# Grouping the products that prepare keys, queries and values in a decoder kernel on one core

## The reference, cut to what matters

```python
# self-attention, 16 heads of 8 features, causal band of 64, relative bias
attn = softmax(where(mask, q @ k.T * scale, -1e30) + bias); y = (attn @ v) @ w_proj.T + b_proj
x = layernorm(x + y)
# cross-attention, 16 heads of 64 features, keys rotated by cos and sin
q = LN(x) @ Wq; k, v = split(LN(ctx) @ Wkv); k = rope(k, cos, sin)
x = layernorm(x + softmax(clip(q @ k.T * scale, -11, 11)) @ v @ Wo + bo)
```

## Time and profile before

| | us |
|---|---|
| median of 3 runs | 1079.42 |
| lowest and highest | 1076.92 and 1081.24 |
| the profiled execution, its own time | 1080.22 |
| its span in the trace | 1078.5 |
| busy: TensorE, VectorE, ScalarE, GpSimd | 932.1, 686.1, 513.8, 503.9 |
| main phase, first `unit(0)` to the start of the last `unit(1)` | 88.7 to 831.4 |
| mean granted clock over the span | 0.938 |

### The profile page before, as it was taken

One profiled execution on the slowest core, in us unless ns is written; L12 is line 12 of the kernel. 1 busy time (PEld: TensorE's weight loads), 2 busy tenths in 40 slices (PEclk: granted clock), 3 DMA queues, 4 the chain that ended last, 5 costly groups with the idle time before them and its releaser, 6 DMA issues.

```text
span 1078.5 us, 22081 instructions
## 1 busy us (share of the span) xinstructions
PE 932.1 (86%) x8504; PEld 660.6 (61%) x8504; DVE 686.1 (64%) x1905; ACT 513.8 (48%) x1446; POOL 503.9 (47%) x637
## 2 busy tenths in 40 slices
PE   3658998999899899989999998999989589999932
PEld 2436665666666666666656665666656379888721
DVE  3355657767776765777577658757689634444467
ACT  3645563565466456536645663564334023333324
POOL 1034356536644653565465456446567211333354
PEclk9989899999999999999999999999999669999955
DMA  7100000000000000000000000000000001222211
GB/s 180 28 1 6 11 1 2 5 12 1 6 11 1 2 6 11 1 7 11 2 1 6 11 2 1 1 2 1 21 1 1 1 7 25 32 33 32 32 12 40
DMA packets 60422, 15.09 MB, mean 14 GB/s; under 512 B 41230, under 2 KB 59678, under 8 KB 60190
## 3 DMA queue, kind: packets, MB, share of 16 engines
q1 hardware_dynamic: 60318, 13.69, 6.0%
HBM read 10.51 MB, written 3.17 MB: 13 GB/s over the span
## 4 chain that ended last, share of the span: by engine, by line
PE 63%; DVE 18%; ACT 7%; POOL 5%; issue 3%; DMA 2%; SPq 2%; POOLq 0%; DVEq 0%
PE score_banks L1906 9%; PE out_bank L1830 8%; PE score_banks L1637 5%; PE bank_a L1618 5%; DVE o_rec L1238 4%; PE score_banks L1844 4%; PE score_banks L1662 3%; DVE prob L1336 3%; PE bank_d L1713 3%; PE score_banks L1639 3%; PE score_banks L1638 3%; PE score_banks L2034 3%; PE out_bank L1813 2%; PE out_bank L1838 2%; PE bank_d L2047 2%
## 5 line engine op out<-in xcount | busy, mean ns | idle before, releaser
L914 ACT ACTIVATE prob<-score_banks 128x1024 f32<-128x1024 f32 x128 | 131.2, 1025 | 165.1 <-PE score_banks L1906 164.8
L694 POOL TENSOR_TENSOR psum<-psum,prob 128x512 f32<-128x512 f32 x64 | 81.7, 1276 | 155.0 <-DVE prob L1336 154.9
L1906 PE MATMUL score_banks<-qh,kr 64*128 64x256 f32 x1024 | 150.1, 413 | 1.7 <-ACT qh L873 1.3
L1238 DVE RECIPROCAL o_rec<-out_bank 128x256 f32<-128x256 f32 x64 | 111.9, 1748 | 26.2 <-PE out_bank L1838 26.2
L692 POOL TENSOR_TENSOR psum<-prob 128x512 f32<-128x512 f32 x64 | 82.9, 1295 | 95.2 <-DVE prob L1336 95.0
L1830 PE MATMUL out_bank<-prob,v 128*64 128x256 f32 x1024 | 124.6, 385 | 1.4 <-DVE on L1239 1.4
L1906 PEld LDWEIGHTS score_banks<-qh,kr 64*128 64x128 f32 x1024 | 91.2, 191 | 40.5 <-issue 30.9
L845 ACT ACTIVATE prob<-prob,neg_max 128x128 f32<-128x128 f32 (+1 forms) x256 | 107.0, 426 | 12.9 <-DVE neg_max L1138 12.9
L1336 DVE TENSOR_SCALAR prob<-prob 128x1024 f32<-128x1024 f32 x128 | 100.5, 785 | 12.9 <-ACT prob L914 12.9
L1830 PEld LDWEIGHTS out_bank<-prob,v 128*64 128x64 f32 x1024 | 67.8, 136 | 46.6 <-issue 17.2
L963 ACT ACTIVATE prob<-score_banks 128x8 f32<-128x8 f32 x255 | 45.3, 178 | 97.5 <-PE score_banks L2034 97.5
(11 more groups left out here) (384 smaller groups left out, 2115.4 us busy)
## 6 DMA issues: line engine op xcount, KB each, us to landing
cb<-in_ctx_dram SPq DMA_DIRECT2D x8, 256.0 KB, 2.9
bias_mask<-bias_scratch SPq DMA_DIRECT2D x1, 1536.0 KB, 7.3
xb<-in_x_dram SPq DMA_DIRECT2D x8, 128.0 KB, 2.1
prob<-in_L_xattn_Wkv_dram SPq DMA_DIRECT2D x1, 1024.0 KB, 7.2
x_scratch<-v SPq DMA_DIRECT2D x16, 64.0 KB, 1.5
bias_mask<-x_scratch SPq DMA_DIRECT2D x16, 64.0 KB
att_scratch<-on SPq DMA_DIRECT2D x16, 64.0 KB, 1.5
prob<-att_scratch SPq DMA_DIRECT2D x16, 64.0 KB, 3.0
```

The costliest lines, as they stand in the source:

```text
L914: s.activation(prob[:, p % 2, 2 * u:2 * u + 2, :].rearrange("p k (h q) -> p h k q", h=2), sc[:, 0:2, :].rearrange("p h (k q) -> p h k q", ...
L1238: link(w.reciprocal(o_rec[:, :], bank[:, T:2 * T]))
L1906: last = mm(sc[:, h, k * T:(k + 1) * T], kr[rows_of, p % 2, kb * P:(kb + 1) * P], qh[rows_of, p % 2, :], start=True, stop=True, skip_group ...
```

## The change

`GROUPED` names the pairs 0, 1, 2, 4, 5 and 6. In these, TensorE issues `keys b` directly behind `keys a` in the first half, and in the second half `queries`, `values 0` and `values 1` directly behind one another, with the slots 2 to 5 after them. VectorE does the sine product of `keys b` ahead of `attended`. ScalarE copies both values behind the queries and ahead of the slots 2 to 5. `prep_targets` numbers the jobs in the new order, which deals the banks anew. Pairs 3 and 7 stay. No instruction is added or removed.

```diff
--- before.py
+++ after.py
@@ -84,6 +84,9 @@
     return job
 
 
+GROUPED = (0, 1, 2, 4, 5, 6)
+
+
 def prep_targets(p, last):
 
     target = {}
@@ -91,9 +94,12 @@
         return {} if last else {"keys a": 1, "values 0": 0, "values 1": 0, "queries": 0, "keys b": 1}
     if p + 2 < PAIRS or not last:
         target["keys a"] = (p + 2) % PAIRS
-    target["queries"] = p + 1
+    if p not in GROUPED:
+        target["queries"] = p + 1
     if p + 2 < PAIRS or not last:
         target["keys b"] = (p + 2) % PAIRS
+    if p in GROUPED:
+        target["queries"] = p + 1
     if p % 2 == 1:
         target["values 0"] = target["values 1"] = (p + 1) // 2
     return target
@@ -934,7 +940,11 @@
                         slots(4, 6)
                     if (b, p, "queries") in JOB:
                         queries(JOB[b, p, "queries"])
-                    if p < PAIRS - 1:
+                    if p in GROUPED:
+                        values_job(0)
+                        values_job(1)
+                        slots(2, 6)
+                    elif p < PAIRS - 1:
                         slots(2, 4)
                         values_job(0)
                         slots(4, 5)
@@ -1348,11 +1358,14 @@
                     clamp(0)
                     slots(0, 1)
                     slots(1, 2)
+                    if p in GROUPED:
+                        keys_job("b")
                     if pair >= 1:
                         attended(pair - 1)
                     clamp(1)
                     slots(2, 3)
-                    keys_job("b")
+                    if p not in GROUPED:
+                        keys_job("b")
                     slots(3, 4)
                     slots(4, 5)
                     if p == 0 and b >= 1:
@@ -1929,13 +1942,20 @@
 
                     unit(0)
                     prep("keys a", prep_keys, "a")
+                    if p in GROUPED:
+                        prep("keys b", prep_keys, "b")
                     slots(0, 1)
                     if pair >= 1:
                         values_of(pair - 1)
                         sum_of(pair - 1)
                     slots(1, 2)
                     unit(1)
-                    if p < PAIRS - 1:
+                    if p in GROUPED:
+                        prep("queries", prep_queries)
+                        prep("values 0", prep_values, 0)
+                        prep("values 1", prep_values, 1)
+                        slots(2, 6)
+                    elif p < PAIRS - 1:
                         prep("queries", prep_queries)
                         slots(2, 3)
                         prep("keys b", prep_keys, "b")
```

## The result

The changed kernel takes **1094.87 us** (median of 4 runs, 1094.31 to 1095.27), the kernel before beside it 1079.44 (1076.92 to 1081.24): a ratio of 1.0152 with an interval of 1.013 to 1.0175. It is 15.4 us slower, as forecast (1096.5 within 1085 to 1106). The profiled execution took 1095.27 us, with a span of 1093.6 us against 1078.5.

A forecast was written before the change was run, and what follows sets the result against it. TensorE was taken to bound the kernel, busy 932.1 of 1078.5 us. Pairs sum to 3.0 us a batch, +21 for seven; 1080.2 + 21 − 2 − 2 = 1097.2, median 1096.5 us, range 1085 to 1106.

The forecast's parts named there:

- First halves +0.70: Every grouped pair before unit(1): the three products of keys b moved there add 0.70 us.
- Pair 1: VectorE sets the pace; subtraction and sine product delay slot 10, its wait splits: net +0.2 us, bounds −0.4 to +0.5.
- Pair 2: Slot 16's turn waits for ScalarE's copy, so only 0.1 us comes back in the second half: net +0.6 us.
- Pair 4: Keys b were hidden in slot 27's wait for ScalarE's copy, so nothing comes back: net +0.7 us, bounds +0.5 to +0.7.
- Pair 5: ScalarE's copies of values delay the chain through slot 32 and the division to slot 35: net +1.5 us, bounds +0.7 to +1.9.
- First and last batch −2: Last batch: moved keys b end a 0.89 us wait; first batch: longer pair 1 waits absorb some; −2 us for both.
- Clock −2: Shorter or split waits in pairs 7 and 1 win back a third of 6.0 us lost at half clock: −2 us.
- The rival "faster": Grouping removes ten border penalties of 0.1 us, 1.0 us a batch, all gained: 1072.5 us, chance 0.05.
- The clock recovers: Rival: all half-clock stretches vanish since no wait lasts 2 us: 1090 us, chance 0.15.
- The clock falls: Rival: pair 1 idles 3.0 us instead of 2.1, some 4 more batches lose 1.5 us each: 1103 us, chance 0.13.
- No difference: Rival: the added 0.7 us is absorbed in the other pairs as in pair 6: about 1081 us, chance 0.07.
- GpSimd's sum is later: Rival: pair 7's second addition waits for pair 6's clamp, behind the sine product: +0.65 us a batch, 1101 us, chance 0.10.

The follow-up runs named there:

- experiment 5: The changed kernel with fewer pairs grouped: 0, 1 and 6 (1068.65 us), 1 alone, 1 and 6, or 0, 1, 4 and 6 (8.8 us above the first).
- experiment 4: The changed kernel with ScalarE copying pair 5's values behind slot 33, TensorE's order untouched: 1094.45 us, ratio 1.0132 to the kernel before.
- experiment 2: The changed kernel with keys b still early, but slots back between queries and values, differing in pairs 1 and 5: 1115.77 us, ratio 1.0319 to the kernel before.
- experiment 3: The kernel before with keys b of pairs 0, 2 and 4 directly behind the queries in the second half: 1091.35 us, ratio 1.0102.

## Why the prediction was right

**Sign, size and mechanism** held: waits took the place of hidden products, +3.2 us a batch against +3.0, and the total was 1.6 us below the forecast. That it is so close is in part luck: the batches took 22.2 us where 21 − 2 was forecast, the clock gave 2.1 more than its term, and code that the change does not touch took 2.8 less. Point by point:

- *First halves +0.70*: 0.78, 0.70, 0.63, 0.70, 0.69, 0.70. Pair 2's is smaller because its `unit(0)` now starts behind slot 10 (experiment 5 has 4.95 there with pair 2 ungrouped).
- *Pair 0* net 0: +0.09. *Pair 1* +0.2: +0.05, two waits of 1.25 and 1.35. *Pair 2* +0.6: +0.62. *Pair 4* +0.7: +0.69, and +0.70 by itself in experiment 5. *Pair 6* eaten by pair 7: its wait went from 2.4 to 1.7.
- *Pair 5* +1.5: +1.73. **The step that failed** is "ScalarE's 1.2 us of copies now stand ahead of it". Slot 32's copy began at +4.05, close to the forecast's, and the copies do stand right ahead of it; but without them (experiment 4) it begins at +3.98, since TensorE's turn of slot 32 is that late by itself. The term was also short by 0.23: slot 35 came at +6.69, not +6.57, and `unit(0)` 0.64 behind it instead of 0.53.
- *First and last batch −2*: the first took 96.98 instead of 96.41, 0.6 more where the others took 3.2 more. Of the 2.6 between, 1.5 is pair 7, 14.02 before with half clock in it and 11.76 after (2.3 less, where the others have 0.7 less), which the forecast did not have; 1.1 is pairs 1 and 2 together, 31.02 before and 30.63 after (the others have 0.7 more), and fits the reason given. The last took **2.4 more**, against the sign of the term. Moving keys b did end the wait of the earlier trace rows (pair 1's second half is 3.76 instead of 5.64), but the other pairs took more than that back. In pair 0 the sum stands 0.70 later on TensorE, the reciprocal waits 0.93 for it and `output` 0.70 for VectorE. Pair 3 takes 13.50 instead of 12.34 and pair 4 9.67 instead of 8.73; in pair 3 values 0 wait 1.86 us for the sine product instead of 1.16, and the half-clock stretch that follows is 6.80 us long, not 3.40. At half its busy time that is about 1.4 us more, an estimate, and TensorE's waits in the batch are 0.9 longer in sum (5.1 against 4.2). The forecast looked at the one wait that ends, at none that begins and not at the clock. The two stretches in the tables, before and after, and the timeline of pair 0:

```profile
802.00:805.40 3.40, 3.40 (x16) 2.25 (x15) 2.41 (x13) 1.05 (x2) 2.17 (x4) 0.51 0.00 0
```

```profile
816.60:823.40 6.80, 6.11 (x22) 4.51 (x22) 3.90 (x14) 2.67 (x4) 3.30 (x4) 0.50 0.00 0
```

```profile
783.53 1.76 DVE L1248 RECIPROCAL o_rec<-out_bank 128x256 f32<-128x256 f32 x1 [0.93 <-PE out_bank L1851]
785.32 0.42 DVE L1249 TENSOR_TENSOR on<-out_bank,o_rec 128x256 f32<-128x256 f32 x1
...
785.80 3.84 PE L1826 MATMUL out_bank<-wo,on 128*128 128x128 f32 x32 [0.70 <-DVE on L1249]
```

- *Clock −2*: −4.1 in the six full batches. They lost 7.5 us before and lose 3.4 now, (100.22 − 98.38) + (99.91 − 98.38), all of it in pair 7 (0.3 of the first is a longer wait there, 1.97 instead of 1.67 us). Start and end of the kernel gave another 0.7 and 2.1, not forecast. The spans close: 6 × 3.2 − 4.1 + 0.6 + 2.4 − 0.7 − 2.1 = 15.3, against 15.1.

*The rival "faster".* The border penalty is in the records, and grouping takes it away there, but no time comes of it. Line 1650 in the changed kernel (count, ns min/median/max, first and last):

```profile
L1650 PE MATMUL score_banks<-wv_s,cn_s x108: 276/283/582, 105.4 to 837.0; 128*128 128x256 f32 x108
L1650 PE MATMUL score_banks<-lat_s,wq_s x55: 279/385/388, 93.1 to 842.3; 128*128 128x256 f32 x55
L1650 PE MATMUL score_banks<-cn_s,wk_s x54: 494/500/735, 89.0 to 830.1; 128*128 128x512 f32 x54
L1650 PE MATMUL score_banks<-cn_s,wkx_s x54: 391/399/629, 89.9 to 822.8; 128*128 128x512 f32 x54
```

A product that enters a group is recorded 0.10 us longer (queries 385 ns, keys a 500) than one inside it (values 283, keys b 399), but TensorE's busy time of a batch is 89.28 before and 89.26 after. And when keys b left the second half of pair 0, it shrank from 6.75 to 6.06, by the three steps of 0.23 of a group and by nothing for a border. The Trainium skill (TensorE: Matmul & The Clock Gate, Step-by-step: what each phase is for) has weights pulled ahead of running products, which would leave no entry penalty. The records of single products speak against it, the time of the batch for it: the forecast's 0.11 was right as a duration and no price.

*The clock recovers* came half true, and with pairs 0, 1 and 6 alone it was true of all six full batches. The Trainium skill (Perfetto Trace Analysis, Matmul Optimizations) wants products back to back in batches, since TensorE scales its power with its utilization. As to the granted clock, the trace agrees in pair 1 with all products grouped; with keys a and keys b alone back to back (experiment 2) it fell there in every batch. As to the time, only pairs in which no other wait was covered by the moved products gain from it. *The clock falls* happened in experiments 2 and 3, not in this change. *No difference* and *GpSimd's sum is later* did not happen: pairs 2, 4 and 5 absorbed nothing, and pair 7's wait became shorter by the whole 0.7.

## What to carry to other kernels

A product that stands alone between steps of a tight chain may be what hides an engine's answer; before moving it to join its like, read pair by pair which wait starts behind it, and group only where none does. A wait that can't be removed is worth splitting: two of 1.3 us kept the clock that one of 2.1 lost in many batches. With pair 1 alone so treated the kernel is 0.5% faster, at an unchanged length of the full-clock batch. Of a step that is moved ahead, ask which turn of the same engine now stands behind it: here TensorE's turn of slot 32 in pair 5, and its sum in the last batch, which no slots follow.

## What the runs showed of the hardware that was not expected

The granted clock is not a matter of one wait's length. These counts are of one profiled execution each. Pair 7's wait of 1.7 us (2.0 in one batch) was followed by 3.40 us at half clock in none of seven batches with 0, 1 and 6 grouped, in two of the changed kernel and in four with pair 5 put back; the wait of 2.08 us in pair 1 in three of six full batches before and in all six of experiment 3. Nor does it follow the idleness of a batch: the changed kernel idles more in pair 5 than the one with pair 5 put back, and fell less often. Each such stretch costs about 1.6 us. In the profiled executions they begin somewhere from 0.6 us before the end of a wait to 1.7 us behind it, and lie over dense work. What exactly decides was not tried and stays open; so does why the part behind the main phase, whose code is unchanged, took 247.1, 244.9 and 246.0 us in the three main kernels.
